# An eight-batch attention and FFN chain: layer 1's attention gets one written step list per group of heads, layer 3's self-attention splits keys and queries on three engines

## The reference

```python
x = x + _L1_xattn_ref(_layernorm(x, axis=-1), ctx_1024, ctx_1024, L1_xattn_Wq, L1_xattn_bq, ...)   # 16 heads of 8, no mask
...
def _msa(x, w_qkv, w_proj):        # layer 3: batches of 256 tokens here, 16 heads of 8
    ...
    attn = jnp.einsum('bhnd,bhmd->bhnm', q, k) * (1.0 / np.sqrt(DK))
    attn = jax.nn.softmax(attn, axis=-1)
    y = jnp.einsum('bhnm,bhmd->bhnd', attn, v)
    y = y.transpose(0, 2, 1, 3).reshape(b, n, d)
    return y @ w_proj
```

## Time and profile before

| | us |
|---|---|
| median of 3 runs | 4298.92 (4298.91 to 4302.66) |
| profiled execution, own time | 4301.44 |
| its span | 4299.7 |
| mean granted TensorE clock | 0.966 |
| PE busy | 4007.4 (93%) |
| DVE busy | 2751.3 (64%) |
| ACT busy | 2777.2 (65%) |
| POOL busy | 864.2 (20%) |

### The profile page before, as it was taken

How to read it: one execution, slowest core, us unless ns; L and a number is a source line. 1 busy time by engine, 2 the same in 40 slices (tenths; PEclk the granted TensorE clock), 3 DMA queues, 4 the chain that set the end, 5 groups by cost and what they waited for, 6 DMA issues and landing times. The chain is left out here.

```text
span 4299.7 us, 72412 instructions
## 1 busy us (share of the span) xinstructions
PE 4007.4 (93%) x26524; PEld 2864.9 (67%) x26524; DVE 2751.3 (64%) x6263; ACT 2777.2 (65%) x4848; POOL 864.2 (20%) x769
## 2 busy tenths in 40 slices
PE   7897899999889999999999999789999999978799
PEld 6654444444467777777777777548888888854467
DVE  7655888888466666566566565465566556548556
ACT  6523667767357667676767677437777777757456
POOL 2100000000000000000000000007777777751100
PEclk9998999999899999999999999899999999989899
DMA  2100433231100000000000000100000000000100
GB/s 72 42 1 26 80 50 51 44 42 15 45 13 1 13 13 1 13 1 13 1 13 13 1 1 1 43 16 9 9 9 9 9 1 1 1 10 1 41 3 8
DMA packets 55898, 78.90 MB, mean 18 GB/s; under 512 B 10164, under 2 KB 47173, under 8 KB 54445
## 3 DMA queue, kind: packets, MB, share of 16 engines
q1 hardware_dynamic: 51084, 67.97, 7.4%
q10 hardware_dynamic: 4464, 6.30, 0.4%
HBM read 51.31 MB, written 4.19 MB: 13 GB/s over the span
## 5 line engine op out<-in xcount | busy, mean ns | idle before, releaser
L2388 POOL TENSOR_TENSOR L3a_p_lo<-L3a_wq,L3a_p_hi 128x512 fp32r<-128x512 f32 (+1 forms) x480 | 625.7, 1315 | 241.0 <-ACT L3a_p_hi L2325 232.2
L1223 DVE CUSTOM_DVE_ANT_0 L2a_sc<-L2a_score,L2a_mask_n 128x804 f32<-128x804 f32 x512 | 500.0, 991 | 211.5 <-issue 194.6
L603 ACT ACTIVATE L1a_work<-L1a_ring 128x1024 f32<-128x1024 f32 x416 | 412.3, 1025 | 164.3 <-PE L1a_ring L435 164.1
L1113 ACT ACTIVATE L2a_pt<-L2a_ring 128x512 f32<-128x512 f32 x768 | 424.5, 597 | 138.4 <-PE L2a_ring L1002 133.3
L717 DVE TENSOR_REDUCE L1a_mx<-L1a_ring 128x2 f32<-128x1024 f32 x384 | 456.5, 1222 | 50.3 <-PE L1a_ring L454 45.6
L1098 ACT ACTIVATE L2a_sc<-L2a_sc,L2a_nb 128x1608 f32<-128x1608 f32 x256 | 418.4, 1636 | 33.9 <-DVE L2a_nb L1228 33.9
L1002 PE MATMUL L2a_ring<-L2a_ident,L2a_sc 128*128 128x128 f32 x3072 | 424.3, 278 | 15.4 <-ACT L2a_sc L1098 9.0
L1002 PEld LDWEIGHTS L2a_ring<-L2a_ident,L2a_sc 128*128 128x128 f32 x3072 | 341.6, 141 | 85.9 <-issue 35.9
L2480 DVE TENSOR_REDUCE L3a_mx<-L3a_ring 128x1 f32<-128x402 f32 (+2 forms) x640 | 316.5, 538 | 120.8 <-PE L3a_ring L2177 113.1
L2324 ACT ACTIVATE L3a_wq<-L3a_ring 128x512 f32<-128x512 f32 (+1 forms) x480 | 284.0, 592 | 148.0 <-PE L3a_ring L2099 104.4
L1017 PE MATMUL L2a_res<-L2a_pt,L2a_v 128*64 128x256 f32 (+1 forms) x3328 | 375.3, 382 | 1.4 <-ACT L2a_pt L1113 1.4
(11 more groups left out here) (743 smaller groups left out, 8713.1 us busy)
## 6 DMA issues: line engine op xcount, KB each, us to landing
L1a_keys<-L1a_k_hi SPq DMA_DIRECT2D x224, 52.0 KB
L1a_kt<-in_ctx_t SPq DMA_DIRECT2D x8, 800.5 KB, 4.4
L2a_ct<-in_ctx_t SPq DMA_DIRECT2D x8, 800.5 KB, 4.3
L1a_keys<-L1a_k_lo SPq DMA_DIRECT2D x112, 52.0 KB
L0a_cx<-in_ctx SPq DMA_DIRECT2D x16, 320.0 KB, 3.9
L3a_cx<-in_ctx SPq DMA_DIRECT2D x16, 320.0 KB, 3.7
L2a_mask_u<-in_mask SPq DMA_DIRECT2D x16, 200.1 KB, 4.5
L1a_scr_q<-L1a_keys SPq DMA_DIRECT2D x3, 1024.0 KB
```

Source lines behind the costliest of these rows:

```text
L603: act.activation(probs[:, (par * NU + u) % c.PS, :, :], ring[tile][:, :, :], ACT.Exp).then_inc(tile_free[tile], 1)
L1113: ins = act.activation(pt[:, t:t + 4, g // 3, q], bank[:, :].rearrange("p (t q) -> p t q", t=4), ACT.Copy)
L1223: dve.tensor_tensor_reduce(sc[:, two, e, w].rearrange("p (k j) -> p k j", k=2), score[e][:, :, 0:CH], mask_n[:, r % 2, w].rearrange("p (k ...
L2388: pool.tensor_tensor(p_lo[0:r, at % PL, 0:W], probs[0:r, at % 2, 0:W], p_hi[0:r, at % PH, 0:W].bitcast(F32), ALU.subtract).then_inc(part_o ...
```

## The change

**Layer 1.** `ORDER` and `SIDE` are replaced by `ORDERS`, four strings, one per group, with the auxiliary steps written in them. A `values` step now is one context tile (`PV = CT`, 13 steps of 4 matmuls for 7 steps of 8). ACT's waits for `pv_ok` count single tiles. The first top of a group in the list does the waits for the DMAs of that group (`opening`). ACT's `result` waits for a `spread` of the batch before in two of the four groups. One top of the group of heads behind (`U4`, `U13`) is pulled into the end of groups 3 and 1.

```diff
-    PV = -(-CT // 2)
+    PV = CT
-    ORDER = """S0 T4 S1 V5 T12 S2 T13 T5 V6 S3 T6 R T7 S4 T8 V0 S5 T9 V1 T10 S6 T11 V2 S7 U0 U1 H S8 S9 V3 U2 S10 W S11 U3 S12 V4"""
-    SIDE = {(0, "T4"): ("key", 0, 1), (0, "T7"): ("key", 1, 1), (0, "T9"): ("key", 2, 1), (0, "T11"): ("key", 3, 1),
...
+    ORDERS = ["S0 key0 V10 S1 T5 S2 V11 V12 T12 R T13 T7 S3 T6 key1 S4 T8 V0 V1 T9 S5 key2 V2 V3 S6 T10 T11 key3 V4 V5 S7 U0 V6 S8 U1 H denominator0 S9 U2 S10 V7 W S11 U3 S12 V8 V9 spread0",
+              "S0 T4 S1 V10 V11 V12 R T13 T12 S2 spread1 T6 S3 T5 project0 T7 S4 T8 V0 V1 S5 T9 V2 V3 T11 S6 T10 V4 V5 S7 U0 value0 U1 H S8 S9 V6 V7 S10 U2 S11 W S12 U3 V8 V9 U13",
+              "S0 T4 S1 V10 V11 T12 S2 T5 S3 V12 T7 R S4 T6 V0 V1 T8 S5 T9 V2 V3 finish0 T10 S6 T11 V4 V5 S7 U0 value1 U1 S8 S9 V6 V7 H U2 S10 W S11 S12 U3 V8 V9",
+              "S0 T4 S1 V10 V11 T13 S2 T12 T6 V12 R T5 S3 value2 T7 S4 T8 V0 V1 S5 T9 V2 T10 value3 S6 T11 V3 V4 U0 S7 U1 V5 S8 H S9 V6 U2 S10 W V7 S11 U3 S12 V8 V9 U4"]
...
             def result(b, par, g):
                 act.wait_ge(pv_ok, b * NG * c.PV + (g + 1) * c.PV)
+                if b and g % 2 == 0:
+                    act.wait_ge(aux_free, c.aux(b - 1, "spread", g // 2) + 1)
                 act.activation(oraw[:, g, :], res[:, 0:S], ACT.Copy).then_inc(oraw_ok, 1)
```

```diff
-                act.activation(q_hi[:, k % 2, :], bank[:, :], ACT.Copy).then_inc(q_ok, 1)
+                for e in range(2):
+                    act.activation(q_hi[:, k % 2, e, :], bank[:, :], ACT.Copy, scale=cols[:, 2 + 2 * e:3 + 2 * e])
...
+            def query_lo(at):
+                n, g = at
+                k = n * NG + g
+                if n:
+                    aux_taken(pool, "query", at)
+                    for e in range(2):
+                        ins = pool.tensor_tensor(queries[:, g, e, span(n)], q_hi[:, k % 2, e, :].bitcast(F32), q_x[:, k % 2, e, :],
+                                                 ALU.add)
+                    ins.then_inc(queries_ok, 1)
...
-            run(dict(scale=scale_of, resid=resid, denominator=denominator))
+            run(dict(scale=scale_of, resid=resid, denominator=denominator, key_lo=key_lo, query_lo=query_lo))
```

More of the change, by code:

```diff
@@ L202, in __init__ @@
+    STEPS = dict(S="scores", T="tops", U="tops", H="shift", W="rows", V="values", R="result")
     def __init__(self):
         self.order = []
-        put = lambda kind, n, off=0: self.order.append((kind, off, n))
         for g in range(self.NG):
[L209 to L223, removed]
-                else:
-                    put("result", *of(-1))
-                if (g, s) in self.SIDE:
-                    put(*self.SIDE[g, s])
+            later = lambda d: ((g + d) % self.NG, (g + d) // self.NG)
+            ended = False
+            for step in self.ORDERS[g].split():
+                name, k = step.rstrip("0123456789"), int(step[len(step.rstrip("0123456789")):] or 0)
+                kind = self.STEPS.get(name, name)
+                G, off = later({"T": 1, "U": 2, "H": 1, "W": 1, "R": -1, "V": 0 if ended else -1}.get(name, 0))
+                if kind in self.AUX and kind != "rows":
+                    self.order.append((kind, 1 if kind in ("key", "value") else -1, k))
+                elif kind == "scores" or kind == "values":
+                    self.order.append((kind, off, G * CT + k))
+                elif kind == "tops":
+                    self.order.append((kind, off, (G, k)))
+                else:
+                    self.order.append((kind, off, G))
+                ended = ended or kind == "result"
+        at = {}
+        for k, (kind, off, n) in enumerate(self.order):
+            if kind == "tops":
+                at[n] = k - off * len(self.order)
+        self.opening = {min((n for n in at if n[0] == g), key=at.get) for g in range(self.NG)}
@@ L441, in tops @@
                 hf, one, ch = piece(i)
-                if i == 0 and not (isinstance(b, int) and b == 0):
+                if n in c.opening and not (isinstance(b, int) and b == 0):
                     if g == 0:
@@ L459, in values @@
                 g, pair = n // c.PV, n % c.PV
-                tiles = [jt for jt in (2 * pair, 2 * pair + 1) if jt < CT]
+                tiles = [pair]
                 for jt in tiles:
@@ L1741, in query_lo @@
                 k = n * NG + g
-                dve.wait_ge(q_ok, k + 1)
-                aux_taken(dve, "query", at)
-                for e in range(2):
-                    ins = dve.scalar_tensor_tensor(queries[:, g, e, span(n)], q_hi[:, k % 2, :].bitcast(F32),
-                                                   cols[:, 2 + 2 * e:3 + 2 * e], q_x[:, k % 2, e, :], ALU.mult, ALU.add)
-                ins.then_inc(queries_ok, 1)
+                if n == 0:
+                    aux_taken(dve, "query", at)
+                    for e in range(2):
+                        ins = dve.tensor_tensor(queries[:, g, e, span(n)], q_hi[:, k % 2, e, :].bitcast(F32), q_x[:, k % 2, e, :],
+                                                ALU.add)
+                    ins.then_inc(queries_ok, 1)
             def tops(at):
```

28 lines of the change are left out of this document (16 added, 12 removed).

## The result

The changed kernel takes 4274.1 us (4273.1 to 4276.7, 4 runs), the kernel before beside it 4300.8 us (4298.9 to 4304.9, 4 runs): ratio 0.9937, 95% interval 0.9925 to 0.9948, 26.7 us gained. Forecast were 4264 us and a range of 4240 to 4290.

What follows compares the result with a forecast made beforehand. PE was taken to bound layer 1, and DVE to be fullest in layer 3's self-attention. Profiled 4301.4 - 22 (layer 1) - 13 (layer 3) = 4266.4 us, less 2.5 for the median: 4264 us, range 4240 to 4290.

Steps and rivals of the forecast that it cites:

- PE bounds layer 1: Layer 1 batch of 80 us: PE steps sum to 74.3 us, 93% of it; 5.7 us are waits.
- U0/U1 to S8: Layer 1, group 0: a values step put between these steps removes 0.7 us of tile wait a batch.
- U2 to U3: Layer 1: distance stays 1.8 us; values steps in groups 0 and 3 remove 2 x 0.48 = 1.0 us a batch.
- the parted tops: Layer 1: T6 and T7, formerly together, are parted in all groups; 1.1 us of other waits a batch go.
- Group 3 and the full DVE: Layer 1, group 3: one more maximum brings DVE to about 17.2 us, what PE needs too; no gain left there.
- Layer 3: Self-attention: moving sums from DVE to POOL gains 15 - 1.8 = 13 us, between ends of 22 gained and 3 lost.
- The waits for maxima: Layer 3, three blocks: PE's 18.2 us of waits for maxima are the gain's ceiling apart from matmul tails.
- The start: Layer 3: ACT runs without a gap there, so three added query copies lose 3 x 0.6 = 1.8 us.
- The port: Layer 3: POOL's sums exclude DVE's second half of `shift`; 2 us of the 13 put down to it.
- My mark for being wrong: Layer 3: wrong if ACT's exponentials no longer wait for PE or L1765's successor grows beyond 0.2 us.
- Rival 4: Layer 3: POOL's sums hold up 24 shifts twice, losing 62 us against 35 gained: 4326 us; chance 0.04.
- The last step of the sum: Whole kernel: the median stands 2.5 us below the profiled execution, turning 4266.4 into 4264 us.

Runs made afterwards that it cites:

- the run with T4 back: Changed kernel with the fifth top moved from the end of group 3 (U4) back to the head of group 0 (T4): 4272.2 us, ratio 0.9924.
- a copy less: Changed kernel without ACT's second rounded copy of a query in layer 3, one copy serving both sums: 4269.8 us, ratio 0.9919.
- the run of layer 3 alone: Kernel before with only layer 3's new splitting, layer 1 as before: 4287.0 us, ratio 0.9957.
- POOL's sums doubled: Changed kernel with each of POOL's 36 layer 3 sums followed by one more unread instruction of nearly the same size: 4284.5 us, ratio 0.9957.
- V7 between in groups 1 and 2: Changed kernel with values step V7 moved from behind V6 to between U2 and U3 in groups 1 and 2: 4268.2 us, ratio 0.9919.

## Why the prediction was right, and where its terms were off

**PE bounds layer 1; its steps can be added up.** Right in the main: 74.3 us of work was forecast, and by the same reading the steps of the changed batch come to 74.6. A cluster of n single values steps costs about 0.14 + 0.43 n us (0.57 at 545.67, 1.00 for two), so a lone single is 0.07 dearer than half of a pair. I had priced it at nothing; the batch, with 30 clusters for 28, pays 0.3.

**The waits.** U0/U1 to S8: 0.7 forecast, gone as described. U2 to U3: forecast to stay 1.8 us everywhere, with a values step in groups 0 and 3. So it did in groups 0 and 1 (1.78 and 1.80). In group 3 it is 2.06, more than the wait for a tile, and group 2 had been read wrongly: there S12 and not U3 takes the tile, and the 1.82 us are found between U2 and S12. And of the 1.0 us booked for the two groups, the half in group 3 was counted against my own sentence that DVE leaves no gain there: group 3 took 18.2 us before and takes 18.3. That is the step of the sum that failed. The 1.1 us for the parted tops came to about 0.9: group 1 20.2 to 19.6 us, group 2 18.4 to 18.1. Group 0 gave 22.9 to 21.8, of which 0.4 is the top that went to group 3. Together 1.8 us an undisturbed batch instead of 2.8, 14 us over eight instead of 22. Not priced at all were the ends: the start takes 1.6 us more and batch 0 gives only 0.4, the last batch with the end gives 6.1 instead of 1.8. Why was not tried. That the phase gave 14.2 us, as eight undisturbed batches would, is a chance sum of these.

**The clock.** Not in my sum at all. Half-clock stretches in five of the batches 1 to 6, one of them twice as long, cost 7.5 us (4 x 1.2 + 2.7); in four of these batches before, 5.7. They make most of the difference between executions of the same lists: the changed layer 1 measured 705.7, 706.0, 701.0, 700.7 and 701.5 us in five executions of the four kernels that share it, and its batches 1 to 6, with five, five, four, three and three stretches, 474.9, 474.9, 472.1, 471.8 and 471.0 us. The rest lies in the start and the end. So the gain of layer 1 is 14 to 19 us, and 22 was too much.

**Group 3 and the full DVE.** 17.2 us of DVE against 17.2 of PE was forecast to leave nothing, and the run with T4 back shows 17.9 us there without the extra top: right, 0.4 us of what was moved.

**Layer 3.** 13 us forecast, 15.6 measured (12.6 to 19.3 over the kernels that share it). That they lie so near is in part luck: 4.5 of the 15.6 us come from the last seven units, where nothing was booked and the clock was higher; the start and the three blocks, which the sum was about, give 11.1. The waits for maxima: 18.2 as the ceiling, 15.7 of it gone. The start: 1.8 lost forecast, 2.5 measured, and 2.2 given back with a copy less. ACT's copies with a factor are 0.69 us each (0.60 before):

```profile
L1634 ACT ACTIVATE L3s_q_hi<-L3s_aux,L3s_cols 128x512 fp32r<-128x512 f32 x32 | 20.4, 692 | 0.8 <-PE L3s_aux L1498 0.5
```

POOL's sums are 1.27 us for the 1.315 of the earlier trace rows, and POOL's busy time grew by 42.8 us for 47. The blocks with sums take 43.8 and 42.7 us, better than the 45 to 47 forecast, but the first one 50.6: the clock took there some of what DVE gave (47.5 us at a clock of 0.96 in the run of layer 3 alone).

**The port.** 2 us booked, at most about 1.6 found. Nearly all of the 3.9 us fell on five of the 128 instructions of the shift, each held 0.3 to 1.1 us. My mark for being wrong, the second half of the shift beyond 0.2 us, was reached by the letter (208 ns for 175) while the layer paid in full; the mark was too near. The rule quoted from the Trainium skill, "SBUF — State Buffer", section "SBUF: two separate sides", is borne out here for the second half, which has two operands in SBUF:

```profile
3935.20 2.54 POOL L1721 TENSOR_TENSOR L3s_queries<-L3s_q_hi,L3s_q_x 128x512 fp32r<-128x512 f32 x2
...
3935.44 1.17 DVE L1786 SCALAR_TENSOR_TENSOR L3s_parts<-L3s_top,L3s_parts 128x4 bf16<-128x4 f32 x2
```

The pair L1786, 0.26 us in the next rows, takes 1.17: its first instruction ends when POOL's first sum does (3936.5). The first half, a `tensor_scalar` with one operand in SBUF, is held too:

```profile
3873.48 2.49 POOL L1721 TENSOR_TENSOR L3s_queries<-L3s_q_hi,L3s_q_x 128x512 fp32r<-128x512 f32 x2 [3.70 <-ACT L3s_q_x L1636]
3874.74 1.34 DVE L1783 TENSOR_SCALAR L3s_parts<-L3s_top 128x4 bf16<-128x4 f32 x2
3876.15 0.26 DVE L1786 SCALAR_TENSOR_TENSOR L3s_parts<-L3s_top,L3s_parts 128x4 bf16<-128x4 f32 x2
```

The pair L1783, 0.25 us elsewhere, ends only when POOL's second sum does (3875.97). I had feared this for L1765's successor alone. That section names `tensor_scalar` among the operations that can run in a mode in which they contend with GpSimd; whether this one ran in it the trace doesn't show. Rival 4 needed 1.5 us a unit to turn the sign; the change put 3.9 us on 32 units, 0.12 each. On the other side the port gives something back: before, five of the sixteen sums of keys stood still behind POOL's wide reciprocal (1.83 to 2.04 us for 0.75), 6.2 us of DVE's time, and with the keys on POOL that is gone.

**The last step of the sum.** 2.5 us were taken off because the median before stood that much below its profiled execution. That was chance of which execution was profiled: the changed kernel's median is 4274.1 us and its profiled execution 4273.5.

## What to carry to other kernels

Where an in-order engine shares a short ring of buffers, count the work between a step and the one that takes its buffer again. Moving a filler from one gap to another can only move the wait (here 0.6 us a batch were lost by it), and a gain is to be booked only where the engine that frees the buffer has room. When you book a gain by place, strike the places that your own count of the other engine has already closed.
Work that moves to GpSimd costs its neighbour too: sum the victim's instructions over the phase (here 16.1 to 20.0 us) and price them at some share, not at zero. And before a variant that is 0.1% better is called better, look how many half-clock stretches its profiled run happened to have.

## What was not expected of the hardware

PE's granted clock falls to half (1.2 for 2.4 GHz) in the middle of a phase in which PE is hardly ever idle. In batch 4 of the changed kernel:

```profile
787.60:791.00 3.40, 3.40 (x26) 1.44 (x23) 2.44 (x3) 2.66 (x4) 1.47 (x1) 0.50 0.46 47
```
```profile
784.68 1.95 PE L511 MATMUL L1a_aux<-L1a_pick,L1a_oraw 128*128 128x4 f32 x16
...
787.12 0.40 PE L435 MATMUL L1a_ring<-L1a_shifted,L1a_keys 64*128 64x512 f32 x2
787.45 1.01 PE L475 MATMUL L1a_res<-L1a_work,L1a_v 128*32 128x256 f32 x8
```

What PE had done just before were the denominator's sixteen matmuls of four columns. Every stretch inside batches 1 to 6 stands behind the denominator, in all kernels, and follows it when it is moved. Whether a given batch has one differs from execution to execution of the same kernel (batches 2, 3, 4, 5, 6 in one, 1, 2, 3, 4, 6 in the other). Two more kernels with the same lists have one in every second batch only: 1, 3, 5 with the three copies, 2, 4, 6 with POOL's sums doubled. In the changed kernel a stretch costs 1.2 us for 3.4 us at half clock and 2.7 for 6.8. In the kernel with V7 between in groups 1 and 2, nothing was changed in the group that holds the denominator, and yet no batch from 1 to 6 had one; why is open, and no kernel without the small matmuls was tried.
